# Feed-forward tiles in two orders by parity, and the next input's transposes in banks of their own

## The reference, cut to what matters

```python
def geglu_ff(x, w1, b1, w2, b2):            # block 0, tanh gelu
    h = jnp.einsum('bne,ef->bnf', x, w1) + b1
    a, gate = (h[..., :DFF], h[..., DFF:])  # DFF = 1280
    h = a * jax.nn.gelu(gate)
    return jnp.einsum('bnf,fe->bne', h, w2) + b2
x = geglu_ff(layer_norm(x, g3, be3), w_ff1, b_ff1, w_ff2, b_ff2) + x
...
h3 = _ln(x, n3_g, n3_b)                     # block 1, exact gelu
proj = h3 @ ff_w1 + ff_b1
a, g = jnp.split(proj, 2, axis=-1)
ff = a * jax.nn.gelu(g, approximate=False) @ ff_w2 + ff_b2
return ff + x
```

## Time and profile before

| | |
|---|---|
| median of 3 runs | 3612.92 us (3609.6 to 3615.88) |
| the profiled execution's own time | 3612.91 us |
| its span in the trace | 3611.0 us |
| mean granted TensorE clock | 0.977 |
| TensorE busy | 3419.9 us (95%) |
| VectorE, ScalarE, GpSimd busy | 1909.7, 1483.3, 677.3 us |

### The profile page before, as it was taken

One profiled execution on the slowest core, in us unless ns is written; L12 is line 12 of the kernel. 1 busy time (PEld: TensorE's weight loads), 2 busy tenths in 40 slices (PEclk: granted clock), 3 DMA queues, 4 the chain that ended last, 5 costly groups with the idle time before them and its releaser, 6 DMA issues.

```text
span 3611.0 us, 38848 instructions
## 1 busy us (share of the span) xinstructions
PE 3419.9 (95%) x15478; PEld 1418.8 (39%) x15478; DVE 1909.7 (53%) x2246; ACT 1483.3 (41%) x2023; POOL 677.3 (19%) x420
## 2 busy tenths in 40 slices
PE   8999999999999999999996899999998999989997
PEld 3334343433334343434443333333333545633332
DVE  3656556565656566661222666666661222556663
ACT  3443434344444535331110555556552112326553
POOL 2433333343333433330000000000000000000000
PEclk9999999999999999999997999999999999979999
DMA  3000000000100000002000000000003000000000
GB/s 109 19 15 15 19 15 15 21 17 21 33 18 15 21 12 15 15 1 57 0 0 24 1 1 1 21 10 5 1 1 80 1 0 23 1 5 5 5 1 30
DMA packets 43554, 60.49 MB, mean 17 GB/s; under 512 B 7408, under 2 KB 31216, under 8 KB 43376
## 3 DMA queue, kind: packets, MB, share of 16 engines
q1 hardware_dynamic: 43376, 58.02, 5.5%
HBM read 55.39 MB, written 2.62 MB: 16 GB/s over the span
## 4 chain that ended last, share of the span: by engine, by line
PE 89%; DVE 5%; issue 3%; ACT 2%; DMA 1%; SPq 1%; POOL 0%; ACTq 0%; DVEq 0%; POOLq 0%
PE bank L463 9%; PE bank L551 9%; PE bank L1033 6%; PE bank L673 5%; PE bank L348 5%; PE bank L1485 4%; PE bank L609 4%; PE bank L958 4%; PE bank L975 4%; PE bank L1487 4%; PE bank L1151 3%; PE bank L612 3%; DVE heads L990 3%; PE bank L644 2%; PE bank L1086 2%
## 5 line engine op out<-in xcount | busy, mean ns | idle before, releaser
L990 DVE TENSOR_REDUCE heads<-bank 128x2 f32<-128x1024 f32 x480 | 587.5, 1224 | 426.9 <-PE bank L975 425.7
L500 DVE TENSOR_REDUCE heads<-bank 128x2 f32<-128x1024 f32 x320 | 390.9, 1222 | 534.9 <-PE bank L488 531.2
L522 ACT ACTIVATE probs<-bank 128x1024 f32<-128x1024 f32 x320 | 327.6, 1024 | 425.8 <-PE bank L468 423.0
L535 POOL TENSOR_TENSOR heads<-heads,probs 128x1024 f32<-128x1024 f32 x160 | 381.2, 2382 | 254.8 <-ACT probs L522 252.2
L463 PE MATMUL bank<-heads 64*128 64x512 f32 x1280 | 361.3, 641 | 0.9 <-ACT probs L522 0.9
L551 PE MATMUL bank<-probs,values 128*64 128x512 f32 x1280 | 345.2, 618 | 0.2 <-ACT probs L522 0.2
L531 POOL TENSOR_TENSOR heads<-probs 128x1024 f32<-128x1024 f32 x80 | 193.1, 2413 | 749.2 <-ACT probs L522 749.2
L958 PE MATMUL bank<-heads 32*128 32x512 f32 x1920 | 306.5, 624 | 5.9 <-ACT weights L1003 3.0
L580 DVE RECIPROCAL rec<-ox 128x128 f32<-128x128 f32 x320 | 280.1, 917 | 7.7 <-ACT ox L573 7.7
L1003 ACT ACTIVATE weights<-bank 128x1024 f32<-128x1024 f32 x238 | 230.6, 1021 | 114.5 <-PE bank L958 113.9
L975 PE MATMUL bank<-heads 32*128 32x512 bf16 x960 | 191.7, 396 | 62.8 <-DVE heads L990 57.9
(11 more groups left out here) (202 smaller groups left out, 4819.2 us busy)
## 6 DMA issues: line engine op xcount, KB each, us to landing
heads<-in_wqk SPq DMA_DIRECT2D x40, 320.0 KB, 2.8
heads<-in_wqk SPq DMA_DIRECT2D x40, 256.0 KB, 2.6
ctx_in<-in_ctx SPq DMA_DIRECT2D x12, 384.0 KB, 3.7
weights<-in_L_xattn_wo SPq DMA_DIRECT2D x2, 1600.0 KB, 11.1
x_res<-in_x SPq DMA_DIRECT2D x4, 640.0 KB, 11.9
out<-x_res SPq DMA_DIRECT2D x1, 2560.0 KB, 8.7
weights<-in_L_xattn_w_ff SPq DMA_DIRECT2D x1, 1600.0 KB, 13.2
weights<-in_L_xattn_ff_w SPq DMA_DIRECT2D x1, 1600.0 KB, 14.5
```

The lines of the kernel that those rows point to most:

```text
L500: nc.vector.tensor_reduce(v["negm"][:, U % 2, qb, :].rearrange("p (g k) -> p g k", g=2)[:, :, 0], M.ROWS[:, :, :], AX.X, ALU.max, negate=T ...
L522: nc.scalar.activation(v["probs"][:, kb, :, :], M.COLS[:, :, :], ACT.Exp, scale=float(r.work[n][0].prm["dh"]) ** -0.5).then_inc(r.sem("exp ...
L535: nc.gpsimd.tensor_tensor(ps, ps, pr[:, k, :, :], ALU.add).then_inc(r.sem("part"), 1)
L990: nc.vector.tensor_reduce(v["negm"][:, tile, qb, 64 * half:64 * half + 64].rearrange("p (g k) -> p g k", g=2)[:, :, at], M.ROWS4[:, :, :], ...
```

## The change

Three things are different in both feed-forward stages.

- **The tile's order.** An even tile stays as it was: four large matmuls, then the pair. An odd tile now begins with the pair, which opens both accumulations, and its large matmuls close them. So an even tile's pair and the next odd tile's pair stand side by side, and so do the large matmuls of an odd tile and of the even tile behind it. In an odd tile `g_ps` is counted by the gate's last large matmul and `a_ps` by the linear half's.
- **The transposes' banks.** They go to `M.XB` (banks 6 and 7) in place of `M.PJ`, and chunks 0 and 1 no longer wait for `ot`.
- **The third chunk's place.** Chunk 2 is issued by `out_pe`, behind output quarter t = 0. The first batch of a stage still does its three chunks at once.

```diff
-        def inputs_pe(pe, s, b):
-
-            hold(pe, xn, after(overall(s, b), TB, TB))
-            k = 0
-            for a, w in CH:
-                w = P
-                if k >= 2:
-                    hold(pe, s.sem("in_evac" + s.tag), after(b - s.first, 3, k - 1))
-                elif b > s.first:
-                    pe.wait_ge(s.sem("ot"), after(b - 1, NF, NF - 1 + k))
+        def inputs_pe(pe, s, b, chunks):
+
+            for c in chunks:
+                if c == 0:
+                    hold(pe, xn, after(overall(s, b), TB, TB))
+                if c == 2:
+                    hold(pe, s.sem("in_evac" + s.tag), after(b - s.first, 3, 1))
                 for t in range(TB):
-                    last = nc.tensor.transpose(M.PJ[k % 2][0:w, t * P:t * P + P], M.xn[:, t, a:a + w], M.ident[:, :])
+                    last = nc.tensor.transpose(M.XB[c % 2][:, t * P:t * P + P], M.xn[:, t, P * c:P * c + P], M.ident[:, :])
                 last.then_inc(s.sem("in_ps" + s.tag), 1)
-                k += 1
...
-                nc.scalar.activation(M.hT[:, c, :], M.PJ[c % 2][:, :], ACT.Identity,
+                nc.scalar.activation(M.hT[:, c, :], M.XB[c % 2][:, :], ACT.Identity,
...
                 last.then_inc(s.sem("y"), 1)
+                if t == 0 and b + 1 < s.first + B:
+                    inputs_pe(pe, s, b + 1, (2,))
...
+        def ff_large(v, bank, f, first):
+
+            for e in range(2):
+                last = nc.tensor.matmul(bank[:, :], v["w1"][:, e, f], M.hT[:, e, :], start=first and e == 0, stop=(not first) and e == 1)
+            return last
+
+        def ff_pair(v, gate, gf, lin, af, first, s):
+
+            g = nc.tensor.matmul(gate[:, :], v["w1"][0:64, 2, gf], M.hT[0:64, 2, :], start=first, stop=not first)
+            a = nc.tensor.matmul(lin[:, :], v["w1"][64:P, 2, af], M.hT[64:P, 2, :], start=first, stop=not first)
+            if not first:
+                g.then_inc(s.sem("g_ps"), 1)
+                a.then_inc(s.sem("a_ps"), 1)
+
...
-            inputs_pe(pe, s, s.first)
+            inputs_pe(pe, s, s.first, range(3))
...
-                    for e in range(2):
-                        nc.tensor.matmul(gate[:, :], v["w1"][:, e, gf], M.hT[:, e, :], start=e == 0, stop=False)
-                    for e in range(2):
-                        nc.tensor.matmul(lin[:, :], v["w1"][:, e, af], M.hT[:, e, :], start=e == 0, stop=False)
-                    nc.tensor.matmul(gate[:, :], v["w1"][0:64, 2, gf], M.hT[0:64, 2, :], start=False, stop=True).then_inc(s.sem("g_ps"), 1)
-                    nc.tensor.matmul(lin[:, :], v["w1"][64:P, 2, af], M.hT[64:P, 2, :], start=False, stop=True).then_inc(s.sem("a_ps"), 1)
+                    if j % 2 == 0:
+                        ff_large(v, gate, gf, True)
+                        ff_large(v, lin, af, True)
+                        ff_pair(v, gate, gf, lin, af, False, s)
+                    else:
+                        ff_pair(v, gate, gf, lin, af, True, s)
+                        ff_large(v, gate, gf, False).then_inc(s.sem("g_ps"), 1)
+                        ff_large(v, lin, af, False).then_inc(s.sem("a_ps"), 1)
                 if b + 1 < s.first + B:
-                    inputs_pe(pe, s, b + 1)
+                    inputs_pe(pe, s, b + 1, range(2))
```

## The result

The changed kernel takes 3582.89 us (median of 6 runs, 3582.12 to 3587.01) against 3612.72 us for the kernel before (median of 6, 3609.6 to 3615.88): a ratio of 0.9919, 95% interval 0.9906 to 0.9932. It is 29.8 us faster where 23.2 were forecast, and lies 1.6 us under the lower end of the range. The profiled execution took 3583.47 us, its span is 3581.2.

The account below looks back on a forecast made before the run. TensorE, busy for 95% of the span, was taken as the bound. Savings of 14.8 (tile order), 6.9 and 1.5 us (batch ends) sum to 23.2, off 3612.91: 3589.7 us, range 3584.5 to 3598.

Parts of the forecast that it names:

- Tiles and changes of row mode: Feed-forward tiles: 72 fewer changes between 128-row and 64-row work, 0.205 us each, save 14.8 us.
- A: Between adjacent pairs: the odd pair's wait for `ot` empties the array, so only odd-to-even joints win; 3597.9 us, chance 0.06.
- B: In the tiles: the 0.41 us belongs to the pair, not the change, so reordering wins nothing; 3604.5 us, chance 0.04.
- C: Odd tiles' opening pairs: halves run one after the other, 34.2 us more; 3623.9 us, chance 0.04.
- The end of a batch: Output starts sooner behind the last tile: 1.15 us in six batches (6.9 us), 0.73 in the last two (1.5 us).
- waited behind the norm: Sign of error: tile 7 waiting for VectorE's product behind the norm after tile 4; about 0.7 us of cover was expected.
- the stage's start: First tile of a feed-forward stage, order kept, low granted clock: no gain taken; feed-forward savings come off the end time.
- The starting point: The time the savings were taken from: the profiled execution's 3612.91 us, also the median of the runs.
- The range: Forecast time from 3584.5 us (run spread of 3.3 us, chunk 2 partly free) up to 3598 us (rival A).

Follow-up runs that it names:

- The moved kernels: Kernel before with 0.86, 1.71 or 2.57 us of matmuls added in s5: 3608.9, 3610.3, 3607.8 us mean; changed kernel with 1.71 us added there: 3587.3 us.
- before + 2.57 us in s5: Kernel before with three overwritten matmuls added ahead of tile 6 in s5's last batch: ratio 0.9995, mean 3607.8 us.
- before + 0.86 us in s5: Kernel before with one overwritten matmul added ahead of tile 6 in s5's last batch: ratio 0.9994, mean 3608.9 us.

## Why the prediction was wrong, point by point

- **Tiles and changes of row mode: right.** Two tiles take 8.98 us, 8.97 forecast. At 0.20 a change, 72 are 14.4 us and not 14.8. Rivals A, B and C are out: no gap between pairs, a pitch that fell by 2.43 with the order alone, halves that start together.
- **The end of a batch: right in kind, 1.2 us too much.** 0.97 for 1.15 in six batches and 0.65 for 0.73 in two, since VectorE starts 0.27 behind TensorE's end and chunk 2 costs 0.51. In all 21.5 us where the sum said 23.2. No tile waited behind the norm: the list of waits has none for it.
- **The step that failed** is the one on the stage's start: "I take nothing there. Stages follow one another through `x_done`, so what a feed-forward saves comes off the end." What a feed-forward saves also moves all stages behind it against the moments at which TensorE's granted clock falls and rises, and these stages last several us more or less by it: s7, with the same records, took 422.8 and 421.6 us in the kernel before and 418.5 and 418.4 in the changed one. The changed kernel came out 27.3 us faster by the means (29.8 by the first medians), 6 to 8 more than its own rows pay for.
- **Whose the 6 us are.** At equal granted clock the changed kernel is 23.1 +- 0.7 us faster; the other 4.2 go with its higher mean clock, 0.9797 where the kernel before has 0.9778. The moved kernels say the same in another way. Beside the line of slope one the kernel before lies 2.2, 1.7 and 5.0 us lower at its three other places in s5, so with its own place it stood 2.2 us above the average of the four; the changed kernel, moved once, lies 2.6 above its line, so it stood 1.3 under the average of two. Taking both out leaves 23.8 us, with an error of 1.1 from the spread of the executions alone; with the places in s2 counted too, the two averages are some 24.6 us apart. So the excess goes with the clock, and about half of it or more belongs to the places at which the two kernels happen to stand, and not to the change as such. The 1.6 us between 23.1 and the rows' 21.5 stay open. The first tiles of s2 and s5 can't be counted on for them: they were fast in both profiles of the changed kernel, but also in the second one of the kernel before, and slow in those of the changed kernel with work added in s2.
- **The starting point** was 3612.91 us, which is 2.6 over the mean of the kernel before in 122 executions. From 3610.3 the same sum gives 3587.1. That part of the miss is the draw of a few executions and no fault of the mechanism.
- **The range** had its lower end from the spread of three runs and from chunk 2. The 122 executions of the same kernel reach from 3602 to 3621 us, so a term of some 4 us for the clock belonged in it on either side. It would have held the result.

## What to carry to other kernels

Group TensorE's work by row mode: put 64-row pairs next to one another, so that every second tile opens its sums with the pair and the others close theirs with it. Each change avoided was worth 0.20 us here (float32, 512 columns, full clock), and it shows in the rows as a load that nothing hides. Cost an edit by the pitch of the loop it stands in, at full clock, and not by the end time alone: on a kernel with slow stage starts the end time moves by several us when a stage merely ends at another moment. To see which it is, set the time of every execution beside its mean granted clock and compare the kernels at equal clock. Or add 1 to 3 us of TensorE work at the place in question and look whether the time follows.

## What the runs showed of the hardware that I had not expected

- The time at the lower clock level (1.2 GHz, granted clock 0.5) behind a stage's start isn't a property of the stage. s7, with the same records, took between 416.2 us (before + 2.57 us in s5) and 428.5 us (before + 0.86 us in s5), at 0.66 and 0.54 in the window from 10 to 50 us.
- Added work need not show in the time: 2.57 us of matmuls in s5 left the kernel at 0.9995 (0.9986 to 1.0004), with a mean granted clock of 0.9796 in place of 0.9778. And 0.86, 1.71 and 2.57 us added in s2 of the changed kernel ended at a span of 3582.4 us in all three profiled executions, where the means rose from 3583.6 to 3587.2.
- The reverse holds for an idle TensorE: 1.8 us of pause ahead of s6 cost 8 us, with 17 us at the lower level behind it.
